# First and third attention of a four-layer kernel: scores negated and scaled by the rotation tables, row minimum as the exponential's bias

## The reference, cut to what matters

```python
# first attention: 32 heads of 16, 4 sequences of 256 tokens
q, k = apply_rope(q, sin, cos), apply_rope(k, sin, cos)
scores = einsum('bnth,bnsh->bnts', q, k) * (1.0 / sqrt(16))
attn = softmax(where(causal, scores, -inf))
# third attention: 32 query heads of 128 on 8 key heads, in four sequences of 256
xq, xk = apply_rope(xq, cos, sin), apply_rope(xk, cos, sin)
scores = einsum('bqhd,bkhd->bhqk', xq, xk) * (1.0 / sqrt(128))
probs = softmax(where(causal, scores, -1e30))
```

## Time and profile before

| | us |
|---|---|
| median of 3 executions | 1591.64 |
| lowest, highest | 1590.28, 1594.16 |
| span of the profiled execution, first to last instruction | 1586.9 |
| PE busy | 1430.3 (90%) |
| DVE busy | 1120.2 (71%) |
| ACT busy | 735.7 (46%) |
| POOL busy | 432.0 (27%) |
| granted PE clock from about 635 to 674 us, one slice of 40 | 0.6 |

### The profile page before, as it was taken

How to read it: one execution, slowest core, us unless ns; L and a number is a source line. 1 busy time by engine, 2 the same in 40 slices (tenths; PEclk the granted TensorE clock), 3 DMA queues, 4 the chain that set the end, 5 groups by cost and what they waited for, 6 DMA issues and landing times.

```text
span 1586.9 us, 26588 instructions
## 1 busy us (share of the span) xinstructions
PE 1430.3 (90%) x9332; PEld 1215.0 (77%) x9332; DVE 1120.2 (71%) x2171; ACT 735.7 (46%) x1996; POOL 432.0 (27%) x328
## 2 busy tenths in 40 slices
PE   4888888869999797899999999999999999958998
PEld 3776767547777585788888988889888988846887
DVE  6686868678999853546776778767687767863554
ACT  3675757532222221425555555555555555532332
POOL 5100000003223370433343241434243342315000
PEclk9999999999999999699999999999999999988999
DMA  6000010113322000210202010020202120010000
GB/s 198 28 1 28 1 57 10 40 41 102 118 79 73 7 14 2 74 34 28 67 28 67 26 33 33 26 66 26 66 26 66 26 66 14 13 47 20 15 13 26
DMA packets 39681, 67.80 MB, mean 43 GB/s; under 512 B 4940, under 2 KB 13799, under 8 KB 39618
## 3 DMA queue, kind: packets, MB, share of 16 engines
q1 hardware_dynamic: 37522, 65.69, 13.2%
q10 hardware_dynamic: 2096, 1.30, 0.3%
HBM read 60.65 MB, written 2.13 MB: 40 GB/s over the span
## 4 chain that ended last, share of the span: by engine, by line
PE 59%; DVE 21%; issue 13%; POOL 3%; ACT 3%; DMA 1%; SPq 0%; POOLq 0%; DVEq 0%; ACTq 0%
PE PS L325 14%; PE PS L327 14%; PE PS L326 14%; DVE E_p L1253 3%; DVE A_mx L1024 2%; DVE E_nb L1244 2%; DVE E_mx L1240 2%; PE PS L1793 2%; DVE A_pT L1011 2%; DVE E_T L1262 1%; PE PS L1776 1%; PE PS L1459 1%; PE PS L1491 1%; POOL E_sw L526 1%; PE PS L1480 1%
## 5 line engine op out<-in xcount | busy, mean ns | idle before, releaser
L325 PE MATMUL PS<-XNH,E_WL 128*128 128x256 f32 x768 | 218.1, 284 | 6.7 <-POOL E_WL L440 5.9
L326 PE MATMUL PS<-XNL,E_WH 128*128 128x256 f32 x768 | 214.4, 279 | 0.0
L327 PE MATMUL PS<-XNH,E_WH 128*128 128x256 f32 x768 | 214.2, 279 | 0.0
L526 POOL TENSOR_TENSOR E_sw<-E_sw,rope2s 128x1024 f32<-128x1024 f32 x64 | 103.3, 1615 | 309.9 <-ACT E_sw L578 309.9
L1240 DVE TENSOR_REDUCE E_mx<-PS 128x4 f32<-128x512 f32 x64 | 60.8, 951 | 139.2 <-PE PS L1779 139.2
L325 PEld LDWEIGHTS PS<-XNH,E_WL 128*128 128x128 f32 x768 | 144.7, 188 | 11.1 <-POOL E_WL L440 8.9
L326 PEld LDWEIGHTS PS<-XNL,E_WH 128*128 128x128 f32 x768 | 144.5, 188 | 1.0
L327 PEld LDWEIGHTS PS<-XNH,E_WH 128*128 128x128 f32 x768 | 144.4, 188 | 0.0
L791 ACT ACTIVATE E_p<-PS,E_nb 128x128 f32<-128x128 f32 (+1 forms) x256 | 103.8, 431 | 85.1 <-DVE E_nb L1244 85.1
L578 ACT ACTIVATE E_sw<-PS 64x256 f32<-64x256 f32 (+1 forms) x128 | 89.5, 699 | 103.8 <-PE PS L327 102.3
L440 POOL TENSOR_TENSOR E_WL<-raw,E_WH 128x512 fp32r<-128x512 f32 x80 | 102.7, 1319 | 124.6 <-ACT E_WH L578 124.6
(11 more groups left out here) (266 smaller groups left out, 4260.3 us busy)
## 6 DMA issues: line engine op xcount, KB each, us to landing
raw<-in_w SPq DMA_DIRECT2D x104, 256.0 KB, 2.9
words<-in_words SPq DMA_DIRECT2D x11, 768.0 KB, 4.3
wo<-in_wo SPq DMA_DIRECT2D x32, 256.0 KB, 3.9
zb<-z_scratch SPq DMA_DIRECT2D x11, 384.0 KB, 5.1
scb<-in_scales SPq DMA_DIRECT2D x11, 384.0 KB, 5.6
X<-in_x SPq DMA_DIRECT2D x8, 256.0 KB, 5.7
SGH<-XNH SPq DMA_DIRECT2D x8, 256.0 KB, 2.7
SGL<-XNL SPq DMA_DIRECT2D x8, 256.0 KB, 2.9
```

The lines of the kernel that those rows point to most:

```text
L325: nc.tensor.matmul(o, sl, mh, start=first, stop=False)
L326: nc.tensor.matmul(o, sh, ml, start=False, stop=False)
L327: return nc.tensor.matmul(o, sh, mh, start=False, stop=last)
L526: nc.gpsimd.tensor_tensor(E_sw[:, heads, :], E_sw[:, heads, :], rope2s[:, :].unsqueeze(1).broadcast_to([P, heads.stop - heads.start, SEQ]) ...
```

## The change

The scale and a sign are put into tables that the kernel already multiplies by. In the first attention the tables get one more index, `is_k`: the query tables are multiplied by -0.25, the key tables by 1. In the third attention both tables are multiplied by 128^(-1/4); the keys get their sign where the rotated sums are split, by an ACT copy with scale -1 and a DVE operation that computes -E_T - QKH. PSUM then holds the negated, scaled scores, and the mask is +1e30. The row minimum of these is what the exponential needs as its bias, so the reduction writes `A_nb` or `E_nb` itself, the exponential has scale -1, and the small product with its wait goes. On DVE 128 executed instructions go (2 in each of 32 turns and 32 slots). On every engine the instructions that stay keep their order. The two first tables are twice as large in memory (128 x 64 numbers in place of 128 x 32).

```diff
-        rope0c = keep("rope0c", [P, 2, D0])
+        rope0c = keep("rope0c", [P, 2, 2, D0])          # rope0s likewise
...
-                nc.gpsimd.tensor_tensor(A_sw[:, :, :], A_sw[:, :, :], rope0s[:, tl, :].unsqueeze(1)...
+                nc.gpsimd.tensor_tensor(A_sw[:, :, :], A_sw[:, :, :], rope0s[:, is_k, tl, :].unsqueeze(1)...
...
-                        act.wait_ge(a["neg"], t * 2 + (tb + 1))
+                        act.wait_ge(a["least"], t * 2 + (tb + 1))
...
-                                                       PS[:, 2 * tb + h % 2, at:at + (tb + 1) * P], ACT.Exp, scale=float(D0) ** -0.5,
+                                                       PS[:, 2 * tb + h % 2, at:at + (tb + 1) * P], ACT.Exp, scale=-1.0,
...
-                        act.wait_ge(e2["neg"], i * 2 + (tb - 1))
+                        act.wait_ge(e2["least"], i * 2 + (tb - 1))
...
-                        copy(QKH[:, heads, :], E_T[:, heads, :], e2["qhi"])
+                        nc.scalar.activation(QKH[:, heads, :], E_T[:, heads, :], ACT.Copy, scale=1.0 - 2.0 * n).then_inc(e2["qhi"], 1)
...
-                        V.tensor_reduce(A_mx[:, 4 * tb:4 * tb + 4],
+                        V.tensor_reduce(A_nb[:, 4 * tb:4 * tb + 4],
                                         PS[:, 2 * tb:2 * tb + 2, :].rearrange("p n (h s) -> p (n h) s", h=2)[:, :, 0:(tb + 1) * P],
-                                        AXIS.X, ALU.max).then_inc(a["mx"], 1)
-                        dve.wait_ge(a["mx"], t * 2 + (tb + 1))
-                        V.tensor_scalar(A_nb[:, 4 * tb:4 * tb + 4], A_mx[:, 4 * tb:4 * tb + 4], -float(D0) ** -0.5, None, ALU.mult)\
-                         .then_inc(a["neg"], 1)
+                                        AXIS.X, ALU.min).then_inc(a["least"], 1)
...
-                    V.tensor_reduce(E_mx[:, 4 * tb:4 * tb + 4],
+                    V.tensor_reduce(E_nb[:, 4 * tb:4 * tb + 4],
                                     PS[:, 3 + 2 * tb:5 + 2 * tb, :].rearrange("p n (h s) -> p (n h) s", h=2)[:, :, 0:(tb + 1) * P],
-                                    AXIS.X, ALU.max).then_inc(e2["mx"], 1)
-                    dve.wait_ge(e2["mx"], i * 2 + (tb - 1))
-                    V.tensor_scalar(E_nb[:, 4 * tb:4 * tb + 4], E_mx[:, 4 * tb:4 * tb + 4], -float(D2) ** -0.5, None, ALU.mult)\
-                     .then_inc(e2["neg"], 1)
+                                    AXIS.X, ALU.min).then_inc(e2["least"], 1)
...
-                    V.tensor_tensor(QKL[:, heads, :], E_T[:, heads, :], f32(QKH[:, heads, :]), ALU.subtract).then_inc(e2["qlo"], 1)
+                    V.scalar_tensor_tensor(QKL[:, heads, :], E_T[:, heads, :], 1.0 - 2.0 * n, f32(QKH[:, heads, :]), ALU.mult, ALU.subtract)\
+                     .then_inc(e2["qlo"], 1)
...
+    turned = np.array([-0.25, 1.0], f32)[:, None, None, None]
+    split = f32(128.0 ** -0.25)
-    hidden = np.where(p[None, :] > p[:, None], -1e30, 0.0)
+    hidden = np.where(p[None, :] > p[:, None], 1e30, 0.0)
...
-        rope2c=cos2.T, rope2s=sin2.T)
+        rope2c=split * cos2.T, rope2s=split * sin2.T)
```

More of the change, by code:

```diff
@@ L65, in build_program @@
         shift_k = keep("shift_k", [P, 1], I32)
-        rope0c = keep("rope0c", [P, 2, D0])
-        rope0s = keep("rope0s", [P, 2, D0])
+        rope0c = keep("rope0c", [P, 2, 2, D0])
+        rope0s = keep("rope0s", [P, 2, 2, D0])
         rope2c = keep("rope2c", [P, SEQ])
@@ L120, in build_program @@
                 A_ps = [A_p, raw[:, 0:3, :].rearrange("p r (n t) -> p (r n) t", t=P)]
-                A_mx = sb(st, "A_mx", [P, 8])
                 A_nb = sb(st, "A_nb", [P, 8])
@@ L222, in build_program @@
                 OL = [sb(st, f"OL{p}", [P, 2, C], F32R) for p in range(2)]
-                E_mx = sb(st, "E_mx", [P, 8])
                 E_nb = sb(st, "E_nb", [P, 8])
@@ L276, in sems @@
             return {n: sem(f"{prefix}_{n}") for n in names.split()}
-        a = sems("a", "stage0 stage1 init proj sw t1 t2 q hi lo tp ev vps vcp sc mx neg exp rec pn pt pe pd pv ot wo_ps x")
+        a = sems("a", "stage0 stage1 init proj sw t1 t2 q hi lo tp ev vps vcp sc least exp rec pn pt pe pd pv ot wo_ps x")
         def prepared(b, g, ago=0):
@@ L302, in build_program @@
         d2 = sems("d", "lo_ps c ax g_ps gh gl tp uh ul up x")
-        e2 = sems("e", "sc mx neg exp rec pn pt phi plo pv ohi olo pq pk sw vt t1 t2 q qhi qlo vtp vhi vlo wo x")
+        e2 = sems("e", "sc least exp rec pn pt phi plo pv ohi olo pq pk sw vt t1 t2 q qhi qlo vtp vhi vlo wo x")
         g3 = sems("g", "in woin s12 s wsh wsl qps m e r sum nps rc mul tp hi lo wo xo out")
@@ L453, in _, with sines @@
             pool.wait_ge(const_in, 16 * 9)
-            def sines(U, tl):
+            def sines(U, tl, is_k):
                 pool.wait_ge(a["sw"], U + 1)
-                nc.gpsimd.tensor_tensor(A_sw[:, :, :], A_sw[:, :, :], rope0s[:, tl, :].unsqueeze(1).broadcast_to([P, H0 // 2, D0]), ALU.mult)\
+                nc.gpsimd.tensor_tensor(A_sw[:, :, :], A_sw[:, :, :], rope0s[:, is_k, tl, :].unsqueeze(1).broadcast_to([P, H0 // 2, D0]), ALU.mult)\
                   .then_inc(a["t2"], 1)
@@ L463, in attend @@
                     if unit:
-                        sines(unit[0], unit[3])
+                        sines(unit[0], *unit[3:])
             for g in FIRST:
                 unit = prepared(-1, g)
-                sines(unit[0], unit[3])
+                sines(unit[0], *unit[3:])
             attend(0)
@@ L791, in l2_slot @@
                             last = nc.scalar.activation(E_p[:, blocks, :].rearrange("p n t -> p (n t)"),
-                                                        PS[:, 3 + 2 * tb + h // 2, at:at + (tb + 1) * P], ACT.Exp, scale=float(D2) ** -0.5,
+                                                        PS[:, 3 + 2 * tb + h // 2, at:at + (tb + 1) * P], ACT.Exp, scale=-1.0,
                                                         bias=E_nb[:, 4 * tb + h:4 * tb + h + 1], accum_out=E_sum[:, 4 * tb + h:4 * tb + h + 1])
@@ L988, in cosines @@
             def cosines(unit):
-                U, _, _, tl, _ = unit
+                U, _, _, tl, is_k = unit
                 dve.wait_ge(a["sw"], U + 1)
                 V.tensor_tensor(A_T1[:, :, :], PS[:, 5, 0:HALF].rearrange("p (h d) -> p h d", h=H0 // 2),
-                                rope0c[:, tl, :].unsqueeze(1).broadcast_to([P, H0 // 2, D0]), ALU.mult).then_inc(a["t1"], 1)
+                                rope0c[:, is_k, tl, :].unsqueeze(1).broadcast_to([P, H0 // 2, D0]), ALU.mult).then_inc(a["t1"], 1)
             def rotate(unit):
@@ L1965 @@
         shift_k=(4 * (p % 8)).astype(np.int32)[:, None], shift_n=np.broadcast_to(4 * np.arange(8, dtype=np.int32), (NF, 8)),
-        rope0c=cos0.reshape(2, P, 16).transpose(1, 0, 2), rope0s=sin0.reshape(2, P, 16).transpose(1, 0, 2),
-        rope2c=cos2.T, rope2s=sin2.T)
+        rope0c=(turned * cos0.reshape(2, P, 16)).transpose(2, 0, 1, 3), rope0s=(turned * sin0.reshape(2, P, 16)).transpose(2, 0, 1, 3),
+        rope2c=split * cos2.T, rope2s=split * sin2.T)
     nc = bacc.Bacc("TRN2", target_bir_lowering=False, num_devices=1)
```

## The result

| | before | changed |
|---|---|---|
| median, us | 1590.96 | 1568.05 |
| lowest to highest, us | 1588.43 to 1594.16 | 1566.07 to 1572.29 |
| span of the profiled execution, us | 1586.9 | 1566.4 |
| DVE busy, us | 1120.2 | 1047.4 |
| PE busy, us | 1430.3 | 1428.1 |

The change makes the kernel faster: ratio 0.9845, 95% interval 0.9825 to 0.9864. That is 22.9 us between the medians and 20.5 us between the two spans. The forecast was 17.3 us and 1574.3, so the direction was right and the size was 3 to 6 us short. In every run whose span is on record the time is 1.8 us above the span; the 3.4 to 7.3 us given above for the kernel before are mostly scatter between executions.

A forecast was written before the change was run, and what follows sets the result against it. DVE's queue between scores and copy was taken to pace the first attention, PE to bound the third. Savings of 12.9 + 4.4 = 17.3 us from 1591.64 gave 1574.3 us, range 1568 to 1584.

The forecast's parts named there:

- 22 x 0.15 = 3.3 us: Third attention: PE's wait before its second transposes vanishes in 22 slots, worth 0.15 each by periods of slots without it.
- 4.4: Third attention, whole saving in us: 3.3 from 22 slots, 0.9 in the first with probabilities, 0.2 in the last.
- The products free what they occupy: First attention: without products, neighbouring reductions and copy overlap by 0.09 us, saving 0.43 us a turn.
- The rival at 0.24: First attention: reductions overlap nothing, so a turn gives only 0.24 us; 11 us in all, 1580.5; chance 0.13.
- The cap of 0.34 by ACT: First attention: ACT's idle time before its copy to qT limits the saving to 0.34 us in 10 turns.
- The last sequence: First attention's end: DVE also unpacks weights and is the bound; one product taking 0.62 frees 0.45 us more.
- the forecast 12.9: First attention, whole saving in us: 21 turns x 0.43, 10 turns x 0.34, and 0.45 more in the last sequence.
- the term 0.9: Third attention, first slot with probabilities: PE waits 1.44 us, and removing the products brings 0.9 us there.
- The last slot: Third attention's end: POOL is quiet and ACT waits for the second product; removing it saves 0.2 us.
- What was added: ACT's negating copy and larger tables cost nothing; QKL as SCALAR_TENSOR_TENSOR takes as long as before, 1.55 us the pair.
- the wait for the next key head's weights: Third attention: PE's 0.85 us wait for each next key head's first weight rest stays, starting from PE's own transposes.
- The clock term of 3 us either way: Between the attentions: a stretch at about 0.6 of full clock can shift bounds; 3 us allowed for all cases.

The follow-up runs named there:

- experiment 4: The changed kernel with one small product by 1.0 put back in each turn of the first attention: 1577.69 us, ratio 0.9894 to the kernel before.
- experiment 1: The kernel before with the change in the first attention alone, the third keeping maxima and products: 1580.57 us, ratio 0.9905.
- experiment 5: The changed kernel timed again, nothing altered, as the measure for three further kernels: 1569.93 us, ratio 0.9847 to the kernel before.
- experiment 6: The changed kernel with ACT rounding the next key head's first two weight tiles earlier: 1556.73 us, against 1569.93 for the changed kernel.
- experiment 7: The changed kernel with DVE making the stack's rests ahead of the reductions in some first-attention turns: 1563.18 us, against 1569.93 for the changed kernel.
- experiment 8: The changed kernel with both earlier weight-tile rounding and the stack's rests ahead of the reductions: 1551.66 us, against 1569.93 for the changed kernel.

## Why the prediction was right in its mechanism and short in its size

The step that failed is the size of one term: what PE makes of the 1.0 us that DVE gains in a slot of the third attention, put at 22 x 0.15 = 3.3 us. The runs show 0.40 in each such slot, and 10.3 us for the third attention as a whole where the forecast had 4.4. The first attention was put 1.5 too high, and the stretches outside the two attentions took 1.2 back. That the sum is only 3.2 short of the 20.5 between the spans is in part luck.

**The products free what they occupy: right.** I took 0.43 for a turn by the overlap of neighbours; the copy moved by 0.42, and the dose of experiment 4 gives half of it for each product. The rival at 0.24 is refuted.

**The cap of 0.34 by ACT: wrong, and small.** I had read ACT's idle 0.34 before `qT` as the room that is left, because its exponentials seemed to start by another clock. In the changed kernel these turns are 0.43 shorter as well, 7.50 to 7.07: ACT's whole chain moved with the turn, presumably since what it waits for (the split of `A_q`) is a step of the same loop; that was not tested by itself. In a loop in steady state, an idle time is no cap unless its far end stands still. Ten turns at 0.09 more would be 0.9 us.

**The last sequence: too high.** I had three turns there at 0.43 and 0.45 for a product held up, 1.7 us, since DVE "is the bound by itself". The first of them went from 7.23 to 7.21, and to 7.21 or 7.22 in experiments 1, 5 and 6, so the products are not on the path there. (With the rests moved in other turns, in experiments 7 and 8, it has 6.90; what sets it stays open.) DVE waits for ACT before its second reciprocal in this turn:

```profile
307.77 0.18 DVE L1031 RECIPROCAL A_rec<-A_sum 128x4 f32<-128x4 f32 x1 [0.55 <-ACT A_p L674]
```

The next two turns changed by -0.19 and +0.17, and the same kernel had 7.07 and 6.47 in its second profile; the granted clock is low for some us near PE's waits in this stretch, in a different turn each time. What these two gain can't be read from the runs. The first attention as a whole gave 11.4 us to its last turn, against the forecast 12.9.

**The third attention: the term 22 x 0.15 was mis-sized.** It measured 0.40 in each loop slot, 21.78 to 21.38. The mechanism was right: the first product was waiting for POOL, DVE came 1.04 earlier, PE's wait before its second transposes went. What failed is the step "what it is worth I read from slots without it". The two slots at 1334.47 and 1356.11 show no wait in brackets, but their twelve transposes last 1.73. Twelve of the same in the first attention of the same trace last 1.47:

```profile
238.10 1.47 PE L1505 MATMUL PS<-ident,raw 128*128 128x128 f32 x12
```

So a wait was hidden in the merged row, and I compared a slot that waited with one that waited a little less. The row of the changed kernel is the undisturbed one:

```profile
1030.61 1.47 PE L1786 MATMUL PS<-ident,E_p 128*128 128x128 f32 x12
```

The bracket hid it as well. Before, the first four transposes and the next eight were two rows:

```profile
1048.04 0.60 PE L1793 MATMUL PS<-ident,E_p 128*128 128x128 f32 x4
```

From there to the start of the eight at 1048.84 it is 0.80. A third of the undisturbed twelve is 0.41 (1.22 from 1030.61 to the next matmul at 1031.83, by three). PE lost 0.39, not the 0.20 in brackets, because the bracket counts from the modelled end of the pipelined matmul before. 0.39 is the 0.40 of the period. With the true size the term is 22 x 0.40 = 8.8 in place of 3.3. The starts of key heads are among these 22, and they gained 0.41 although their own wait of 0.85 stayed. What the term left out are the four slots that seemed to have no wait: each gained 0.25, the 0.26 hidden in its merged row. One place gave some of it back: the start of the first key head took 23.85 where it was 23.14, because ACT's wait for the sixth weight tile's transfer was 3.74 and not 2.77, and PE waited 1.10 for `OL` behind it. That is no effect of the change as far as the traces show, for experiment 1, with the third attention as before, has 4.08 and 24.45.

**The first slot: the term 0.9 was right as far as it went.** PE's wait went from 1.44 to 0.58:

```profile
703.78 0.66 PE L1786 MATMUL PS<-ident,E_p 128*128 128x128 f32 x4 [0.58 <-DVE E_p L1245]
```

The period fell by 1.87. The other 1.0 goes with the clock. In the 10 us behind this slot's waits it was granted 0.83 before (0.50 from 721 to 723 us, which is the lower of its two levels, 1.2 GHz, and full speed from 724 us) and 1.00 after; the columns are the stretch, its length, busy times as in the earlier trace rows, and the clock:

```profile
720.00:730.00 10.00, 9.86 (x62) 8.83 (x62) 4.75 (x7) 5.21 (x11) 3.86 (x4) 0.83 0.09 29
708.00:718.00 10.00, 9.62 (x74) 8.76 (x72) 4.44 (x7) 6.18 (x11) 5.04 (x4) 1.00 0.21 59
```

The period is so in every profile of this study: 21.55 and 21.57 in the two with the locked product, which both have a stretch of low clock there, and 19.68 to 19.89 in the eight without, which have none.

**The last slot** got longer, 18.65 to 19.80, where I forecast 0.2 off. PE waits 2.39 for `OL` there in both, but in the 10 us around this wait the clock was 1.00 before, 0.83 and 0.85 in the two profiles of the changed kernel, and 1.00 again in experiment 6, which has 18.39. Of the ten profiles the three with full clock there have 18.39 to 18.65, and the seven with a low stretch 19.02 to 19.94. With the third attention as it was before, experiment 1 is one of the seven, with 19.49. So the change alone is not what lengthens it; what sets the clock there stays open.

**What was added** cost nothing, as forecast, and the wait for the next key head's weights stayed at 0.85. The clock term of 3 us either way was of the right size: the stage after the first attention differs by 2 between two profiles of one kernel, and by 4 with experiment 1.

The sum by measured terms: 11.4 in the first attention. 2.0 from there to the sixth slot: 1.9 in the first slot and 0.6 in two others, less 0.7 at the first key head, and 0.2 ahead of the third attention. From the sixth slot on 16 slots x 0.40, three of the last key head x 0.25 and six starts of a key head x 0.41, less 1.2 in the last slot: 8.5. And 1.4 given back at the end: 20.5.

## What to carry to other kernels

When a tiny operation shows a length of 2 us beside another engine's work, price what waits for its end, and ask which memory it reads: moving four numbers to PSUM gave the same in each loop slot as removing the instruction. Before taking "a slot without the wait" as the measure, compare the length of its merged matmul row with the same shape elsewhere in the trace, from start to start; waits hide in merged rows and in the modelled ends. When an instruction leaves the path, look again at the waits that you expect to stay: the 0.85 us left at each of seven key heads was worth 1.12 each, and the edit that took it away also hid a transfer worth 1.8.

## What the runs showed of the hardware

A small TENSOR_SCALAR from SBUF to SBUF is held by a GpSimd instruction to its end (2.04 us beside 2.40), and the same with a PSUM source is not (0.16 beside 2.39). A reduction that reads PSUM keeps its time beside it (1224 ns in the 30 of 32 slots where most of it lies beside POOL's sines). A minimum over PSUM takes as long as a maximum (1224 and 1210 ns for 128x1024, 691 and 692 for 128x512). A SCALAR_TENSOR_TENSOR with two SBUF sources in f32 takes 1.216 us for 128x1024, a TENSOR_TENSOR 1.217. Two independent reductions overlap by about 0.09 us (the second starts 0.60 behind the first's start, which lasts 0.69), like other VectorE operations here. The granted clock can drop behind a wait of PE, and then costs more than the wait: at the first slot it dropped behind a wait of 1.44 in both profiles that have it and in none of the eight with at most 0.80, and took 1.0 us beside the 0.86 saved. No rule follows from this, for behind the wait of 2.39 in the last slot it dropped in seven profiles of ten.
